# One chunk further ahead for GpSimd's product of attention outputs and reciprocals

## The reference, cut to what matters

```
qkv = x @ W_qkv.T                           # 16 heads of 16
attn = softmax(causal(q @ k.T) / 4) @ v
x = layernorm(x + attn @ W_proj.T)
h = silu(x @ wg.T) * (x @ wu.T)             # 768 hidden, weights int / 127
x = layernorm(x + h @ wd.T)
```

## Time and profile before

| | us |
|---|---|
| Median of 3 runs (lowest, highest) | 1343.06 (1338.88, 1343.3) |
| The profiled execution, whole | 1337.92 |
| Its span in the trace | 1335.4 |
| TensorE busy | 1236.8 (93%) |
| VectorE busy | 1078.9 (81%) |
| ScalarE busy | 873.6 (65%) |
| GpSimd busy | 383.4 (29%) |

### The profile page before, as it was taken

The page is one execution under the profiler, slowest core; times in us unless marked ns, Lnnn a source line. Parts: engine busy times, 40 slices in busy tenths (PEclk is TensorE's granted clock), DMA queues, the critical chain, the costliest instruction groups (busy, mean ns, idle before and its releaser), DMA issues.

```text
span 1335.4 us, 28651 instructions
## 1 busy us (share of the span) xinstructions
PE 1236.8 (93%) x11348; PEld 593.9 (44%) x11348; DVE 1078.9 (81%) x1526; ACT 873.6 (65%) x1734; POOL 383.4 (29%) x464
## 2 busy tenths in 40 slices
PE   4999988999999999999999989999989898989897
PEld 2665643333333333333333333333355656565554
DVE  5687768989889988999988988988357777777776
ACT  2655557888888888888878778788734343333333
POOL 3000002212222132132221222221235555554544
PEclk7999989999999999999999999999989999999999
DMA  5798521221312433223122123120031332323221
GB/s 196 238 294 246 179 88 50 68 80 51 96 52 63 110 104 96 68 57 93 50 67 83 50 62 87 50 67 27 17 107 64 96 94 90 101 84 107 80 63 48
DMA packets 130293, 124.36 MB, mean 93 GB/s; under 512 B 47456, under 2 KB 101216, under 8 KB 130160
## 3 DMA queue, kind: packets, MB, share of 16 engines
q1 hardware_dynamic: 130160, 122.54, 31.0%
HBM read 71.04 MB, written 50.86 MB: 91 GB/s over the span
## 4 chain that ended last, share of the span: by engine, by line
PE 67%; DVE 11%; ACT 7%; POOL 6%; issue 4%; DMA 3%; SPq 1%; POOLq 0%; DVEq 0%; ACTq 0%
PE ps L1321 18%; PE ps L1304 12%; PE ps L1386 11%; DVE row_max L971 6%; PE ps L1224 6%; PE ps L1207 5%; PE ps L1338 4%; ACT probs L840 4%; PE ps L1229 4%; POOL h_lo L735 3%; PE ps L1251 2%; POOL v_sb L712 2%; DMA q_stack<-max_rows 2%; PE ps L1297 2%; SPq L555 1%
## 5 line engine op out<-in xcount | busy, mean ns | idle before, releaser
L971 DVE TENSOR_REDUCE row_max<-ps 128x2 f32<-128x1024 f32 (+1 forms) x512 | 567.1, 1152 | 42.6 <-PE ps L1229 25.6
L840 ACT ACTIVATE probs<-ps 128x512 f32<-128x512 f32 (+1 forms) x1024 | 506.7, 589 | 96.6 <-PE ps L1304 96.3
L707 POOL TENSOR_SCALAR_AFFINE_SELECT probs<-probs 128x512 f32<-128x512 f32 x256 | 162.8, 637 | 624.2 <-ACT probs L840 534.5
L1321 PE MATMUL ps<-probs,v_ones 128*32 128x512 f32 (+3 forms) x3072 | 328.7, 500 | 10.2 <-issue 8.9
L1304 PE MATMUL ps<-q_stack,k_stack 50*128 50x512 f16 (+1 forms) x1024 | 309.6, 371 | 15.3 <-DMA q_stack<-max_rows 10.4
L1224 PE MATMUL ps<-k_stack,q_stack 48*128 48x512 f16 (+3 forms) x1536 | 306.1, 329 | 11.3 <-DVE row_max L971 10.7
L874 ACT ACTIVATE silu<-ps 128x512 f32<-128x512 f32 x96 | 57.4, 597 | 197.3 <-PE ps L1386 197.3
L1304 PEld LDWEIGHTS ps<-q_stack,k_stack 50*128 50x128 f16 x1024 | 88.5, 93 | 211.0 <-ACT probs L840 174.5
L1229 PE MATMUL ps<-above,one_of_half 64*128 64x64 bf16 (+1 forms) x2048 | 165.8, 203 | 0.0
L735 POOL TENSOR_TENSOR h_lo<-h_sb,h_hi 128x512 f16<-128x512 f32 x96 | 119.4, 1250 | 150.7 <-ACT h_hi L882 150.7
L968 DVE TENSOR_REDUCE row_max<-ps 128x4 f32<-128x1024 f32 (+1 forms) x128 | 122.3, 955 | 34.0 <-PE ps L1229 33.2
(11 more groups left out here) (125 smaller groups left out, 1449.4 us busy)
## 6 DMA issues: line engine op xcount, KB each, us to landing
x_sb<-in_L_attn_x SPq DMA_DIRECT2D x32, 512.0 KB, 5.2
qk_parts<-parts SPq DMA_DIRECT2D x64, 256.0 KB, 3.5
attn_t<-o_sb SPq DMA_DIRECT2D x64, 256.0 KB, 2.8
q_stack<-qk_parts SPq DMA_DIRECT2D x192, 64.0 KB, 2.3
k_stack<-qk_parts SPq DMA_DIRECT2D x192, 64.0 KB, 2.3
v_rows<-v_sb SPq DMA_DIRECT2D x16, 512.0 KB, 3.2
v_flat<-v_rows SPq DMA_DIRECT2D x32, 256.0 KB, 3.5
v_sb<-attn_t SPq DMA_DIRECT2D x32, 256.0 KB
```

The costliest lines, as they stand in the source:

```text
L707: pool.affine_select(out=tile, in_=tile, compare_op=ALU.is_ge, fill=0.0, base=0, pattern=[[0, HG], [1, P]], channel_multiplier=-1).then_in ...
L840: act.activation(tile[:, j, 0:w], ps[:, 4 + use % 3, 0:w], ACT.Exp, scale=scale_of_batch).then_inc(exp_done, 1)
L971: dve.tensor_reduce(row_max[:, half, :, p, qt], banks[:, :, 0:w], AX.X, ALU.max).then_inc(s_free, 1)
L1321: last = pe.matmul(ps[32 * j:32 * j + 32, 7, c0:c0 + w * P], v_ones[n % 2][:, kt, j, :], probs[(NS * n + s) % RING][:, j, 0:w * P], start= ...
```

## The change

The product that GpSimd makes at the end of chunk c is that of chunk c + 3, where it was that of chunk c + 2. The product of chunk 2 is made ahead of chunk 0. The wait for `out_ready` stays as it was. SyncE's list, and those of TensorE, VectorE and ScalarE, are the same.

```diff
                 if has_prev:
                     inverse_deviation(1, ln2_step, c - 1)
-                if c + 2 < NCH:
+                if c + 3 < NCH:
                     if has_prev:
                         pool.wait_ge(out_ready, c)
-                    scale_attn(c + 2)
-
+                    scale_attn(c + 3)
+
+            scale_attn(2)
             chunk_c(0, False, True)
```

## The result

| | before | after |
|---|---|---|
| Median of 4 runs, us | 1340.97 (1337.83 to 1343.3) | 1404.88 (1397.63 to 1408.63) |
| Profiled execution, its span, us | 1337.92, 1335.4 | 1404.29, 1401.7 |
| Mean granted TensorE clock | 0.985 | 0.966 |

The change makes the kernel slower by a ratio of 1.0472, with a 95% interval of 1.0422 to 1.0522. 1406.6 us was forecast.

The account below looks back on a forecast made before the run. Bound: the per-chunk chain of waits through GpSimd's product, 22.47 us a turn. Terms 63.2 - 1.3 + 1.85 + 5 = 68.7 us on the profiled 1337.92 gave 1406.6 us, range 1385 to 1428.

Parts of the forecast that it names:

- The wait that replaces the old one: At GpSimd's product, c from 1 to 12: waits for a load held behind a store, 5.27 us more a turn, 63.2 us.
- The landing, 11.55 us after zero: Zero is the product's start before the change; load bytes end at 11.0, release takes 0.55, so the product starts at 11.55.
- the 1423 us: Time forecast if the release after a load's last byte took the page's 2 us instead of 0.55: 17 us longer.
- `h_lo`, `h_lo`, `rstd` end to end: GpSimd behind the late product: these run without idle gaps, some 0.1 apart, ending at 17.54 instead of 12.27.
- The rest of the turn: From the end of the first layernorm's `rstd` to the next product: no slack, so its 10.20 us stay.
- TensorE's 1.28 us: TensorE's projection wait for the product: gone in all 13 chunks, but shortening only chunk 14's turn, -1.3 us.
- The second sign: In the changed profile, gate and up of block 5 and the transposes each wait about 3 us instead of the projection.
- Chunk 0, +1.85: Chunk 2's product, made ahead of chunk 0, waits for its load and delays `h_lo` and `rstd`: +1.85 us, once.
- The clock, +0.4 a chunk: TensorE's clock may halve after idling, slowing the transposes to the low part: between 0 and 22 us, 5 us taken.

Follow-up runs that it names:

- the new list alone: Kernel before the change with only SyncE's list reordered, each load ahead of the store it stood behind: 1339.88 us, ratio 0.9991.
- plain rows: Changed kernel with the product's four load parts reading plain blocks of 128 rows: 1356.35 us; with x and store also behind those parts: 1349.36 us.

## Why the prediction was right, point by point

**The wait that replaces the old one.** Right, and shown by removing it: load ahead of store gives 1325 us, the new list alone nothing, GpSimd's own wait for the rows nothing in the changed kernel.

**The landing, 11.55 us after zero.** 13.41 us of idle, less the 1.50 that GpSimd idled ahead of the product before, is 11.9. The bytes' end and the release, windows around one product of the changed kernel:

```profile
1190.70:1200.70 10.00, 10.00 (x46) 5.70 (x44) 6.41 (x16) 3.40 (x6) 0.00 (x0) 1.00 0.62 187
1200.70:1202.30 1.60, 1.52 (x8) 0.69 (x8) 0.14 (x1) 0.94 (x2) 0.00 (x0) 1.00 0.45 132
1202.30:1202.70 0.40, 0.40 (x3) 0.00 (x1) 0.00 (x0) 0.27 (x1) 0.00 (x0) 1.00 0.15 51
1202.70:1203.40 0.70, 0.10 (x1) 0.00 (x0) 0.00 (x0) 0.00 (x0) 0.00 (x0) 1.00 0.00 0
```

The bytes end about 1202.6 and the product starts at 1203.40: 0.8 us for the release, and 0.8 in the mean of the twelve, where 0.55 was taken from a cast at the program's start. The 2 us that the page "DMA: Bandwidth & Descriptors" of the Trainium skill, in the anatomy of one DMA, puts mostly on this receipt are more than was measured, and the 1423 us that they would have made were not measured either; that section describes a DMA that GpSimd issues, and these are SyncE's. The size of the load was read from the trace, not understood: I took 11.0 us of traffic as the time of 2 MB. The 11.9 us are 4.2 to the first packet of the four parts, 6.9 for the parts with 8 heads outermost, and 0.8 for the release. The same page of the Trainium skill, in its rules for kernel authors, says that an outermost dimension below 16 confines a DMA to at most as many engines; the share near 0.5 agrees, and the plain rows, 0.89, show what it costs here, 3.6 us a turn (27.61 less 24.00).

**`h_lo`, `h_lo`, `rstd` end to end: 5.99 us from the product's start.** They took 1208.92 - 1203.40 = 5.52: the two `h_lo` lasted 2.26 together, and the gaps of 0.1 that I had put between the instructions aren't there. The rest of the turn, 10.20 forecast, was 10.18 (27.61 less 11.91 less 5.52). Here two misses nearly cancel, 0.36 too little for the landing and 0.47 too much behind it. A turn: 27.61 against 27.74 without the clock. Twelve make 61.7 us against 63.2.

**TensorE's 1.28 us come off in chunk 14 only.** Right: from `rstd` of the second layernorm at 1353.71 to the next, at 1374.88, it is 21.17 us, where before a turn was 22.47. The wait is gone from all 13, and in twelve TensorE waits 50.2 us for `hidden` instead, 4.2 us each, where 3 or more were forecast. The second sign that I gave, 3 us of waiting ahead of the transposes, did not come: 7.8 us in 9 turns, at most 1.2 each, since gate and up of block 5 ran later and at half clock and filled that time.

**Chunk 0, +1.85.** The end of its `rstd`, counted from the stage's first transposes, is 992.40 - 973.85 = 18.55 against 987.76 - 971.04 = 16.72: 1.83 later. Two misses cancel in it: the product started 13.0 us after those transposes instead of 12.5, and what follows it was 0.5 shorter.

**The clock, +0.4 a chunk.** Mis-sized: 0 in the twelve turns. It does fall in each, as the windows show for the turn at 1207:

```profile
1207.00:1211.00 4.00, 3.27 (x8) 1.19 (x9) 2.71 (x3) 1.21 (x2) 4.00 (x4) 0.50 0.00 0
```

but gate and up of block 5 run there, which end 0.7 us ahead of the layernorm on the chain, and TensorE is back at full clock by the low transposes. A turn less its wait is 14.2 us in the changed kernel, where the clock falls in each of the twelve, and in the two with plain rows, where it falls in four and in three of them. Where it did cost is chunk 0, for which I had forecast no clock. From the high to the low transposes:

```profile
996.63 0.88 PE L1372 MATMUL ps<-ident_f,x_hi_rows 128*128 128x128 f16 x8 [2.24 <-ACT x_hi_rows L864]
...
1000.49 0.61 PE L1372 MATMUL ps<-ident_f,x_lo_rows 128*128 128x128 f16 x8
```

3.86 us against 2.21 in the kernel before, 1.65 more, once.

The sum in the spans: 61.7 + 1.83 + 1.65 - 1.28 = 63.9, and 2.8 by which attention ended later in this execution (973.85 against 971.04), are 66.7; the spans differ by 66.3. Those 2.8 us are not the change's, whose instructions come later. Of the 68.7 forecast, 5 stood for a clock that cost 1.65. So the mechanism was right, and that the number came within 2.3 us of the profiled 1404.29 is in part luck: a clock term 3.35 too large stood against 2.8 us of attention that no term foresaw.

## What to carry to other kernels

When work is moved to the next buffer ahead, look for what its load waits for in the list that issues it: a load behind a store in one in-order queue inherits the store's wait, and the kernel before shows no wait there at all. The price can be read beforehand, as the time from that event to the end of the bytes, plus the release and less what slack the work behind it had; here that gave 5.27 us a turn, and 5.14 were measured. And a wait that no data need may keep two engines out of each other's way; take it out only with a run.

## What the runs showed of the hardware

- One GpSimd product with two inputs of 128x1024 in float32 beside four VectorE instructions of 128x256 makes these take 909 ns each instead of 409:

```profile
L1061 DVE TENSOR_SCALAR z_sb<-z_sb,mean_var,rstd 128x256 f32<-128x256 f32 x44 | 37.4, 909 | 5.8 <-POOL rstd L691 5.8
```

- Four DMAs of 256 KB with 8 heads outermost take 6.9 us from first packet to last at a DMA share near one half; the same 1 MB in plain rows takes 3.4 us and lands 3.7 us sooner (13.41 less 9.75).
- 1 MB of other traffic moved from in front of these four DMAs to behind them brought their landing only 0.7 us forward (13.41 less 12.72): behind them it still moved beside them, and they took 8.8 instead of 6.9 us.
- TensorE's clock fell to half in all twelve turns, within or just behind a wait of 4.2 us in the mean for `hidden`, and the turn was no longer for it.
